# Query path of the second layer: once for four batches ahead of the attention loop, through DRAM, with the scores over three PSUM banks

## The reference, cut to what matters

```python
q_hk = (hidden_q @ Wq.T).reshape(Bv, Sv, H, K)
q_big = jnp.einsum('bshk,hkq->bshq', q_hk, w_kc_q)                # 192 per head
q_big = _apply_rope(q_big, sin_q[None, :, None, :], cos_q[None, :, None, :])
kv_r = _apply_rope(kv_c, sin_k[None], cos_k[None])
q_r = jnp.einsum('bshq,hqr->bhsr', q_big, W_qr)
k_r = jnp.einsum('bld,hdr->bhlr', kv_r, W_kr)
attn = jax.nn.softmax(jnp.einsum('bhsr,bhlr->bhsl', q_r, k_r), axis=-1)
ctx_c = jnp.einsum('bhsl,bld->bhsd', attn, kv_r)
ctx_lat = jnp.einsum('bhsd,hkd->bhsk', ctx_c, w_kc_kv)
```

## Time and profile before

| | |
|---|---|
| median of 3 runs | 905.37 us |
| the three runs | 898.53, 905.37, 906.08 us |
| span of the profiled execution, first to last instruction | 903.0 us |
| TensorE busy | 826.4 us, 92% |
| VectorE, ScalarE, GpSimd busy | 585.3, 397.2, 453.2 us |
| granted TensorE clock, mean of the span | 0.966 |

### The profile page before, as it was taken

One profiled execution on the slowest core, in us unless ns is written; L12 is line 12 of the kernel. 1 busy time (PEld: TensorE's weight loads), 2 busy tenths in 40 slices (PEclk: granted clock), 3 DMA queues, 4 the chain that ended last, 5 costly groups with the idle time before them and its releaser, 6 DMA issues.

```text
span 903.0 us, 15604 instructions
## 1 busy us (share of the span) xinstructions
PE 826.4 (92%) x5844; PEld 606.6 (67%) x5844; DVE 585.3 (65%) x1133; ACT 397.2 (44%) x883; POOL 453.2 (50%) x465
## 2 busy tenths in 40 slices
PE   4998879999998799999999999999999999999883
PEld 3566656788887667677667677676767766765442
DVE  3437864213358675677878778778787787786545
ACT  2248852222231454544544454454354454444441
POOL 3000002800041187768776876776776776567630
PEclk9979996999999899999999999999999999999986
DMA  9532022789810100000000100000000000000000
GB/s 212 187 123 89 2 67 79 261 299 317 299 46 10 35 1 12 18 10 10 19 10 1 31 10 2 10 26 7 10 23 10 10 6 10 2 16 10 2 13 11
DMA packets 42168, 52.28 MB, mean 58 GB/s; under 512 B 12230, under 2 KB 35704, under 8 KB 41836
## 3 DMA queue, kind: packets, MB, share of 16 engines
q1 hardware_dynamic: 41068, 49.63, 17.5%
q0 software_dynamic: 1024, 1.64, 0.6%
HBM read 45.80 MB, written 5.36 MB: 57 GB/s over the span
## 4 chain that ended last, share of the span: by engine, by line
PE 68%; DVE 13%; ACT 7%; DMA 5%; issue 5%; SPq 1%; POOL 0%; POOLq 0%; ACTq 0%; DVEq 0%
PE ps L1197 14%; PE ps L1209 10%; PE ps L1177 7%; PE ps L1116 6%; PE ps L1121 3%; PE ps L1232 3%; DMA xs<-xs_scratch 3%; PE ps L1042 3%; PE ps L994 3%; PE ps L1143 3%; ACT sm L1465 2%; PE ps L1055 2%; DVE xyz L1947 2%; DVE xyz L1943 1%; PE ps L893 1%
## 5 line engine op out<-in xcount | busy, mean ns | idle before, releaser
L614 POOL TENSOR_TENSOR acc<-acc,pt 120x800 f32<-120x800 f32 (+1 forms) x157 | 299.1, 1905 | 94.4 <-ACT pt L1674 61.4
L1674 ACT ACTIVATE pt<-ps 120x400 f32<-120x400 f32 (+1 forms) x384 | 190.1, 505 | 222.5 <-PE ps L1197 211.6
L1976 DVE TENSOR_REDUCE nm<-ps 128x1 f32<-128x482 f32 (+1 forms) x336 | 213.7, 655 | 100.3 <-PE ps L1177 98.1
L1197 PE MATMUL ps<-qh,khl 128*120 128x400 f32 (+1 forms) x384 | 157.9, 411 | 11.1 <-ACT pt L1674 8.3
L1209 PE MATMUL ps<-pt,kv 120*64 120x400 f32 (+1 forms) x768 | 143.8, 510 | 0.0
L1177 PE MATMUL ps<-khl,qh 128*128 128x482 f32 (+1 forms) x336 | 131.6, 393 | 5.3 <-DVE nm L1976 4.6
L1197 PE MATMUL ps<-ql,kh 65*120 65x400 f32 (+1 forms) x384 | 134.3, 350 | 0.0
L1197 PEld LDWEIGHTS ps<-qh,khl 128*120 128x120 f32 (+1 forms) x384 | 70.9, 185 | 58.6 <-issue 32.4
L1209 PEld LDWEIGHTS ps<-pt,kv 120*64 120x64 f32 (+1 forms) x768 | 51.9, 138 | 65.8 <-issue 55.8
L636 POOL TENSOR_TENSOR rstd<-veps,mhalf 100x1 f32<-100x1 f32 (+2 forms) x20 | 13.4, 670 | 158.1 <-DVE veps L1808 114.6
L1197 PEld LDWEIGHTS ps<-ql,kh 65*120 65x120 f32 (+1 forms) x384 | 71.3, 186 | 5.1
(11 more groups left out here) (277 smaller groups left out, 1246.0 us busy)
## 6 DMA issues: line engine op xcount, KB each, us to landing
egu<-_L_ffn_gate_up_proj_dram SPq DMA_DIRECT2D x14, 1024.0 KB, 6.0
edn<-in_L_ffn_down_proj_dram SPq DMA_DIRECT2D x14, 512.0 KB, 7.1
spread<-inv_scratch SPq DMA_DIRECT2D x30, 100.0 KB, 2.7
craw<-in_ctx_dram SPq DMA_DIRECT2D x8, 360.0 KB
wo_n<-in_L_xattn_Wo_dram SPq DMA_DIRECT2D x1, 2048.0 KB, 10.5
wq_n<-in_L_xattn_Wq_dram SPq DMA_DIRECT2D x1, 2048.0 KB, 8.0
xs_scratch<-zero SPq DMA_DIRECT2D x1, 1792.0 KB, 9.9
xs<-xs_scratch SPq DMA_DIRECT2D x14, 128.0 KB, 6.1
```

The lines of the kernel that those rows point to most:

```text
L614: nc.gpsimd.tensor_tensor(total[r, :, :], before[r, :, :], pt[j % PT_BUF][r, :, :], ALU.add).then_inc(p_added, 1)
L1197: last = mm(ps[0:key_rows(t), k % 2, 0:HT], lhs[:, keys], rhs[:, HT * a:HT * a + HT], start=first, stop=not first)
L1674: nc.scalar.activation(pt[j % PT_BUF][0:rows, k % 2, :], ps[0:rows, k % 2, 0:HT], ACT.Exp).then_inc(p_ready, 1)
L1976: nc.vector.tensor_reduce(nm3[0:w, i, n:n + 1], ps[0:w, 3 + m % 2, 0:MN], AX.X, ALU.max).then_inc(m_reduced, 1)
```

## The change

The query path of the second layer leaves the loop. Ahead of it stand `QUADS` = 8 groups ("quads"); quad `n` makes 4 heads for 4 batches at once, 400 columns per matmul. `q_tail` makes numbers 128 to 191 of two heads, `q_main` numbers 0 to 127 of one, `q_latent(n - 1)` the 64 numbers of the quad before. The rotation of the tail moves to POOL (`rope_tail`), fed by copies on ACT (`keep_tail`); DVE rotates the main part. `keep_q` and `low_q` write high and low parts to staging tiles, SP stores them to a DRAM scratch (`store_q`, four transfers per quad with 800-byte pieces) and loads them per unit into one of `QBUF` = 3 buffers (`load_q`, three transfers of 64 rows of 3,200 bytes), two units ahead. x has to be normalised and turned for four batches before quad 0 and for the others in quads 1 and 2. The maxima of unit 0 stand in quads 4 to 6, behind each `q_main`, and wait for the loaded query of unit 0. POOL starts `add_weights` only when all stores have landed.

In the loop `q_big`, `rope`, `q_latent`, `keep_q`, `low_q` and `turn_x3` are gone. Scores rotate over banks 0, 1 and 7; the sums move to bank 6 and the gate to banks 5 and 6. A few slots of the feed-forward part move by one to six.

The core of the diff:

```diff
+HB = B // 2
+QUADS = 2 * NU // HB
+QBUF = 3
+SCORE_BANK, GATE_BANK, SUM_BANK = (0, 1, 7), 5, 6
+MAIN_BANK, TAIL_BANK, LATENT_BANK = (0, 1), (6, 7), (2, 5)
+TERNARY_IN, X3_IN, MAX_IN = (0, 0, 2, 2, 3, 3), (1, 1, 2, 2), (4, 5, 6)
...
+        def store_q(sp, n):
+
+            g, p, e = quad(n)
+            sp.wait_ge(q_hi, 2 * n + 2)
+            sp.wait_ge(q_lo, 2 * n + 2)
+            heads = q_dram.rearrange("(g b p) l d (a e n) -> g p l a e d b n", g=2, b=HB, p=PAIRS, a=2, e=2)
+            for l, src in enumerate((qhi[e], qlo[e])):
+                for a in range(2):
+                    sp.dma_start(heads[g, p, l, a, e],
+                                 src[CD * a:CD * a + CD, :, :, :].rearrange("d b i s -> d b (i s)").bitcast(F32)).then_inc(q_stored[e], 16)
+
+        def load_q(sp, u):
+
+            n = 2 * PAIRS * (u // PAIRS // HB) + 2 * (u % PAIRS)
+            for e in range(2):
+                sp.wait_ge(q_stored[e], 64 * (n // 2 + 1))
+            if u == QBUF - 1:
+                sp.wait_ge(latent_done, 2 * QUADS)
+            elif u >= QBUF:
+                sp.wait_ge(s_done, LANE * (u - QBUF + 1))
+            for p in (0, CD):
+                sp.dma_start(qh[u % QBUF][p:p + CD, :].bitcast(F32), q_dram[u, 0]).then_inc(ld_q[u % QBUF], 16)
+            sp.dma_start(ql[u % QBUF][0:CD, :].bitcast(F32), q_dram[u, 1]).then_inc(ld_q[u % QBUF], 16)
...
-            place_max(sp, 0)
+            for n in range(4):
+                store_q(sp, n)
+            load_q(sp, 0)
+            load_q(sp, 1)
             sp.wait_ge(fq_turned, 6)
             sp.dma_start(lnw_b[:, :], lnw.rearrange("(a n) -> a n", a=1).to_broadcast([S, F1])).then_inc(ld_lnw, 16)
+            store_q(sp, 4)
+            store_q(sp, 5)
+            place_max(sp, 0)
+            store_q(sp, 6)
+            store_q(sp, 7)
             for u in range(NU):
                 b = u // PAIRS
+                if u + 2 < NU:
+                    load_q(sp, u + 2)
...
+            def rope_tail(n, a, i):
+
+                m = 4 * n + 2 * a + i
+                pool.wait_ge(tail_kept, m + 1)
+                if n >= 2:
+                    pool.wait_ge(latent_done, 2 * n - 2)
+                nc.gpsimd.tensor_tensor(zt[m % 8][:, :].rearrange("p (b q) -> p b q", b=HB), tail2[i][:, :].rearrange("p (b q) -> p b q", b=HB),
+                                        ropeq[:, 2, :].unsqueeze(1).to_broadcast([128, HB, S]), ALU.mult).then_inc(z_ready, 1)
+
+            for n in range(QUADS):
+                for a in range(2):
+                    for i in range(2):
+                        rope_tail(n, a, i)
+            pool.wait_ge(main_done, 4 * QUADS)
+            pool.wait_ge(z_ready, 4 * QUADS)
+            nc.gpsimd.memset(kh1[1][CD:CD + 1, :].bitcast(F32), 1.0).then_inc(tails_set, 1)
+            pool.wait_ge(tails_set, 3)
+            for e in range(2):
+                pool.wait_ge(q_stored[e], 64 * QUADS // 2)
...
+            def q_tail(n, a):
+
+                g, p, e = quad(n)
+                if a == 0:
+                    pe.wait_ge(x3_kept, HB * (g + 1))
+                if n:
+                    pe.wait_ge(tail_kept, 4 * (n - 1) + 2 * a + 2)
+                h = 2 * HG * p + HG * a + 2 * e
+                for c in range(DC):
+                    last = mm(ps[:, TAIL_BANK[a], 0:HT], wqt[:, c, h:h + 2, :].rearrange("p h q -> p (h q)"),
+                              x3T[:, c, HT * g:HT * g + HT], start=c == 0, stop=c == DC - 1)
+                last.then_inc(tail_done, 1)
+
+            def q_main(n, a, i):
+
+                g, p, e = quad(n)
+                m = 4 * n + 2 * a + i
+                if m >= 2:
+                    pe.wait_ge(rope_done, m - 1)
+                h = 2 * HG * p + HG * a + 2 * e + i
+                for c in range(DC):
+                    last = mm(ps[:, MAIN_BANK[i], 0:HT], wqb[:, c, h, 0:128], x3T[:, c, HT * g:HT * g + HT],
+                              start=c == 0, stop=c == DC - 1)
+                last.then_inc(main_done, 1)
+
+            def q_latent(n):
...
-                    pe.wait_ge(q_lo, u + 1)
-                if k >= 2:
-                    pe.wait_ge(p_ready, k - 1)
-                if k % LANE == PHASE and u:
-                    pe.wait_ge(sums_kept, u)
+                    pe.wait_ge(ld_q[u % QBUF], 48 * (u // QBUF + 1))
+                if k >= len(SCORE_BANK):
+                    pe.wait_ge(p_ready, k - len(SCORE_BANK) + 1)
                 keys = slice(key_start(t), key_start(t) + key_rows(t))
-                for lhs, rhs, first in ((khl[b % 2], qh[u % 2], True), (kh1[b % 2], ql[u % 2], False)):
-                    last = mm(ps[0:key_rows(t), k % 2, 0:HT], lhs[:, keys], rhs[:, HT * a:HT * a + HT],
+                for lhs, rhs, first in ((khl[b % 2], qh[u % QBUF], True), (kh1[b % 2], ql[u % QBUF], False)):
+                    last = mm(ps[0:key_rows(t), SCORE_BANK[k % len(SCORE_BANK)], 0:HT], lhs[:, keys], rhs[:, HT * a:HT * a + HT],
...
+            for n in range(QUADS):
+                q_tail(n, 0)
+                q_tail(n, 1)
+                if n:
+                    q_latent(n - 1)
+                for a in range(2):
+                    for i in range(2):
+                        q_main(n, a, i)
+                        if n in MAX_IN:
+                            for c in range(MC):
+                                if c // 7 == MAX_IN.index(n) and c % 7 // 2 == 2 * a + i:
+                                    max_chunk(0, c)
+                for t in range(6):
+                    if TERNARY_IN[t] == n and n < 2:
+                        turn_ternary(t)
+                for b in range(HB, B):
+                    if X3_IN[b - HB] == n:
+                        turn_x3(b)
+                for t in range(6):
+                    if TERNARY_IN[t] == n and n >= 2:
+                        turn_ternary(t)
+                if n == MAX_IN[-1]:
+                    turn_max(0)
+            q_latent(QUADS - 1)
...
-                    if u + 2 < NU and f < 2 and x in QB_AT:
-                        for part in range(2):
-                            q_big(u + 2, f, 2 * QB_AT.index(x) + part)
...
-                        if f == 2 and u + 2 < NU:
-                            q_latent(u + 2)
...
+            def rope(n, a, i):
+
+                m = 4 * n + 2 * a + i
+                dve.wait_ge(main_done, m + 1)
+                if n:
+                    dve.wait_ge(latent_done, 2 * n)
```

More of the change, by code:

```diff
@@ L270, in build @@
         assert cursor[0] <= after_qb
+        cursor[0] = after_keys
+        xn3 = [place(f"xn3_{i}", [S, D]) for i in range(2)]
+        qhi = [place("qhi0", [128, HB, 2, S], F32R)]
+        qlo = [place("qlo0", [128, HB, 2, S], F32R)]
+        assert cursor[0] <= after_qb
+        cursor[0] = after_qb
+        qhi += [place("qhi1", [128, HB, 2, S], F32R)]
+        qlo += [place("qlo1", [128, HB, 2, S], F32R)]
+        assert cursor[0] <= after_fw
         cursor[0] = after_qb
@@ new lines, in q_main @@
+            def q_main(n, a, i):
[9 more added lines that the diff above has]
+            def q_latent(n):
+                g, p, e = quad(n)
+                pe.wait_ge(rope_done, 4 * n + 4)
+                pe.wait_ge(z_ready, 4 * n + 4)
+                if n:
+                    pe.wait_ge(q_lo, 2 * n)
+                else:
+                    pe.wait_ge(k_kept, 3)
+                for i in range(2):
@@ L1215, in sum_weights @@
                 pe.wait_ge(p_added, (KT - 1) * (u + 1))
-                pe.wait_ge(p_ready, min(LANE * (u + 1) + PHASE, SLOTS * B))
+                b, p = (u + 1) // PAIRS, (u + 1) % PAIRS
+                if p == 0 and b >= 2:
+                    pe.wait_ge(gated, 2 * (b - 1))
+                elif p and b:
+                    pe.wait_ge(x3_ready, b)
                 for a in range(2):
-                    last = mm(ps[CD * a:CD * a + CD, 0, 0:HT], ones[0:KP, :], acc[u % 2][:, a, :], start=True, stop=True)
+                    last = mm(ps[CD * a:CD * a + CD, SUM_BANK, 0:HT], ones[0:KP, :], acc[u % 2][:, a, :], start=True, stop=True)
                 last.then_inc(sums_done, 1)
@@ L1652, in _ @@
                 keep_keys(0, j)
-            keep_x3(0)
-            keep_q(0)
-            for n in range(3):
-                keep_ternary(n)
-            keep_q(1)
-            keep_ternary(3)
-            keep_max(0)
-            keep_x3(1)
-            keep_ternary(4)
-            keep_ternary(5)
+            for b in range(HB):
+                keep_x3(b)
+            for n in range(QUADS):
+                keep_tail(n, 0)
+                keep_tail(n, 1)
+                if n:
+                    keep_q(n - 1, 0)
+                    keep_q(n - 1, 1)
+                for t in range(6):
+                    if TERNARY_IN[t] == n and n < 2:
+                        keep_ternary(t)
+                for b in range(HB, B):
+                    if X3_IN[b - HB] == n:
+                        keep_x3(b)
+                for t in range(6):
```

(18 more changed lines are left out.)

385 lines of the change are left out of this document (175 added, 210 removed).

## The result

The kernel before takes 905.73 us (median of 4, 898.53 to 906.46), the changed one 925.79 (median of 4, 921.89 to 930.58): 1.024 times as long, 95% interval 1.018 to 1.030. Measured again beside the first experiments it was 923.54 against 905.92, ratio 1.024 (1.019 to 1.028). From here on all medians and ratios leave out executions more than 1.5% above the fastest of their kernel. Every ratio is to the kernel before, measured beside the run, and has its 95% interval behind it; it is not the quotient of the two medians and can differ from it by up to 0.4%.

A forecast was written before the change was run, and what follows sets the result against it. TensorE bounds the loop. First scores at 403.5 us (97.4 later), batches summing to 487 against 569.4, and a tail of 27.5 give a 918 us span; with 2.4 to the median, 920 us, range 894 to 938.

The forecast's parts named there:

- The costs ahead of the loop: Ahead of the loop: eight quads of 12.25 us plus late start and waits, loop starting 97.4 us later at 403.5.
- What leaves the loop: On TensorE, six `q_big` parts and one latent product per unit, plus `turn_x3`: 15.3 us less per batch.
- What comes back: At unit starts and inside phases TensorE waits for DVE, returning 4 of 15.3 us; a batch takes 62 us.
- The 1 us at the other boundary: At the unit boundary with `hidden` and `max_h`, TensorE loses about 1 us waiting for DVE.
- The lock: DVE and POOL share a port pair exclusively; `L2017` took 1.21 us against 0.35, so denser loops would lengthen boundary chains.
- POOL bounds the loop: Rival, in the loop: POOL's work and waits make 65 us per batch, 935 us; chance 0.13 together with the stores.
- Batch 0, 55 us: Loop's first batch: 67.65 - 15 + 2.5 = 55 us, the ring of eight tiles covering most of POOL's late start.
- Batch 1, 59: Loop's second batch: 71.3 - 15.3 + 3 = 59 us.
- The last batch: Batch 7, end of the loop: 30 + 33, with a half for the new start 63.5 us.
- The third score bank: In the last batch, saves waits for ACT: 0.5 us in the sample's unit (last but one), 1 in the last.
- The waits do not come back: Rival, at unit starts: TensorE runs on without DVE waits, 895 us, or 907 with half; faster 0.18, within 1% 0.27.
- The stores: Rival, ahead of the loop: stores outlast a quad's 12.25 us, each stretching some 3 us, 940 us; 0.13 with POOL.

The follow-up runs named there:

- POOL quiet: POOL's additions on 8 of 400 columns from a unit's third key tile: on the changed kernel 889.70 us, ratio 0.986; on the kernel before 898.52 us, ratio 0.995.
- the second profile: The profiled execution of the changed kernel run again with nothing edited, span 914.6 us; that run's median was 923.54 us, ratio 1.024.

## Why the prediction was right, and where it was not

- *The costs ahead of the loop, +97.4 us.* Measured +97.3 from the first `shared_out`. Near their forecast, in brackets, are: quad 0 at 278.4 (278), the wait for the load 8.17 (7.5), the slow clock behind it (2; 10.2 with the wait by the run with the early load, against 9.5), the last maxima's turning 1.86 (1.4), the last latent product 1.15 (1.2). Others are not, and cancel. The third `q_main` and its successor wait 0.87 and 0.33 us (2.5). The 3 us in quads 5 and 6 and the 0.3 us ahead of each of seven latent products are not there: none of those waits is over 0.1 us. And the 21 chunks of the maxima, put in with 0.21 us each as in the loop (4.4), took 0.39 each from start to start in the run with the early load, 8.3. That the way to the loop came out to 0.1 us is luck in this part. POOL's additions, put at 1.8 us at most, take 1.9 to 2.0, and nothing hung on it. First scores at 404.6, forecast 403.5.
- *What leaves the loop, 15.3 us per batch.* Right to half a microsecond: 72.7 - 57.9 = 14.8 with POOL quiet in both kernels, and what the third score bank gives is in it.
- *What comes back, 4 us per batch, a batch of 62.* The size is right (61.9 in two of the middle batches, 61.8 in the mean of the five), at slot 3 of the second unit, 2.1 us for 2.2. The 1 us at the other boundary and the 0.8 us inside the phases were not there. In their place stood, against the run with a quiet POOL, 0.65 us in the first unit, at its end, where TensorE waits 0.9 us for the joined maxima (`nmx`) and 0.3 with POOL quiet, and up to 1.3 us of slow clock behind a wait of only 2 us, which I had not counted. So the sum of 4 is in part luck. And the cause is another: I had put it down to the length of DVE's chain. The run with shorter chains gained nothing, the run with a quiet POOL gained all of it, and the run with `xn4` in PSUM and `hq` moved got most of it back with nothing left out.
- *The lock.* The prediction named it as a part of the rival that POOL bounds the loop. It was already in my sum, as 1.21 us in the earlier trace rows, without my seeing that this was the part that could be removed. The Trainium skill, page SBUF — State Buffer, section "SBUF: two separate sides", says that a DVE operation in a 2-port mode and one of GpSimd exclude each other for the whole instruction; the page VectorE: DVE Perf Modes, section "Why PSUM operands drop a tier", that an operand in PSUM rules that mode out. The runs agree with both: 1.21 us in SBUF, ending 0.15 us behind an addition of POOL, 0.49 in PSUM and 0.35 in SBUF with POOL quiet.
- *Batch 0, 55 us.* It took 50.1. I had taken 15 us off 67.65 and added 2.5 for waits that did not come; TensorE's busy time fell by 17.7, and the clock in that stretch rose from 0.95 to 1.00. *Batch 1, 59.* It took 64.6, and 62.3 in the second profile: the backlog of POOL from its late start, which I had let the ring cover, makes DVE wait 2.0 us for POOL's root and TensorE 3.8 for `nm` and 1.8 for `acc`. The two batches cancel, by luck.
- *The last batch, "30 + 33, with a half for the new start".* This term failed, and it makes nearly all of the 8 us by which the loop was missed: 71.1 us. The prediction read nothing off the moved slots of the last batch. There `turn_hq` now stands at slot 25, ahead of `turn_xq`, and waits 2.46 us for DVE's `hq`, which stands behind the whole quantising; a second wait at slot 45 is 2.2 (4.3 in the second profile), the clock of the last unit 0.74. In the run with the early load and the bank at the maxima, where DVE writes `hq` ahead of the quantising, the batch takes 61.9. The second wait is missing in the three runs with two score banks. It goes with the lock: ahead of it stands DVE's product over 1024 columns (L2153), which takes 2.35 us or more in every run of the changed kernel that has the wait at 2.2 to 4.3 us, and 0.74 in those three. That is 1.6 us of it; the rest is open. With POOL quiet the last batch takes 59.4.
- *The third score bank, 0.5 and 1 us.* Mis-sized: 0.8 us in each first unit of a middle batch, 4 to 7 in the loop. In the last batch, where I had put it, it gave nothing: with two banks that batch was 5 to 6 us shorter.
- *The rivals.* "The waits do not come back" is false for the kernel as it is. The stores kept pace, 2.9 to 3.4 us for 200 KB each. "POOL bounds the loop" is right in batch 1. In the middle batches POOL does not bound, since a batch takes 58.7 us with all of its work; by the lock it is what lies behind the 4 us that I had put down to DVE, and nothing came on top of them, where this rival had 3 more per batch.

## What to carry to other kernels

Work that is taken off the engine that bounds may have been the cover of another pair's conflict: before counting it as gain, read what the other engines do under it, and whether one of their instructions takes longer than the same one elsewhere in the trace (here 1.21 us and 0.35). Where a duration depends on when a neighbour's instruction ends and not on its own columns, shortening it gives nothing; move its operand to PSUM, or move it to where the neighbour is idle, and look which instruction inherits the wait. And when a load waits behind stores in one queue, issue it behind the stores that it needs.
